# First attention of an eight-block kernel: the scores are computed once, lessened by the row minimum and turned by transposes

## The reference, cut to what matters

```python
q = einsum('ed,bdw->bew', Wq, qp) + bq[:, None]      # 64 rows = 8 heads of 8
k = einsum('ed,bdw->bew', Wk, qp) + bk[:, None]
val = einsum('ed,bdw->bew', Wv, vp) + bv[:, None]    # vp: patches of the context
scores = einsum('bhdi,bhdj->bhij', qh, kh) / sqrt(8)
scores = where(mp[:, :, None, :] > 0, scores, -1e9)
attn = softmax(scores, axis=-1)
o = gelu(einsum('bhij,bhdj->bhdi', attn, vh), approximate=False)
out = (einsum('de,bew->bdw', Wo, o) + bo[:, None]) * masks
```

## Time and profile before

| | |
|---|---|
| median of 3 runs (lowest, highest) | 1655.13 us (1654.13, 1655.79) |
| the profiled execution's own time | 1655.96 us |
| its span, first to last instruction | 1654.2 us |
| busy in the span: PE / DVE / ACT / POOL | 89% / 59% / 33% / 32% |
| mean granted TensorE clock | 0.974 |
| first attention: first score matmul / last copy of outputs | starts at 56.6 us / starts at 357.7 us |

### The profile page before, as it was taken

The page is one execution under the profiler, slowest core; times in us unless marked ns, Lnnn a source line. Parts: engine busy times, 40 slices in busy tenths (PEclk is TensorE's granted clock), DMA queues, the critical chain, the costliest instruction groups (busy, mean ns, idle before and its releaser), DMA issues.

```text
span 1654.2 us, 20269 instructions
## 1 busy us (share of the span) xinstructions
PE 1477.4 (89%) x6854; PEld 1055.1 (64%) x6854; DVE 981.1 (59%) x2158; ACT 547.8 (33%) x1414; POOL 531.9 (32%) x531
## 2 busy tenths in 40 slices
PE   0788888877888989999899998899999999999898
PEld 0344444434766677676678776777777777777555
DVE  2565666655768334888322245677777777777543
ACT  1223222233342213454323113334434334434332
POOL 4100000004523232341312113545545545443163
PEclk9999999999999979999899999999999999999799
DMA  5111111112313210010111104111111111110001
GB/s 157 53 39 37 33 32 33 28 36 90 96 58 102 64 51 1 8 33 1 39 39 51 39 1 147 32 58 51 46 58 51 46 58 51 46 48 4 7 1 51
DMA packets 63481, 77.52 MB, mean 47 GB/s; under 512 B 7138, under 2 KB 34018, under 8 KB 63252
## 3 DMA queue, kind: packets, MB, share of 16 engines
q1 hardware_dynamic: 62416, 74.99, 14.9%
q10 hardware_dynamic: 964, 1.25, 0.2%
HBM read 57.34 MB, written 10.49 MB: 41 GB/s over the span
## 4 chain that ended last, share of the span: by engine, by line
PE 70%; DVE 12%; issue 5%; POOL 4%; SPq 4%; DMA 3%; ACT 2%; POOLq 0%; DVEq 0%; ACTq 0%
PE bank L423 15%; PE bank L428 14%; PE bank L427 14%; SPq L910 3%; PE bank L2331 3%; PE bank L1961 2%; PE bank L2309 2%; PE bank L1950 2%; PE bank L2224 2%; DMA ring_l<-k 2%; PE bank L1959 2%; PE bank L2206 2%; PE bank L490 1%; DVE xn L1807 1%; PE bank L2318 1%
## 5 line engine op out<-in xcount | busy, mean ns | idle before, releaser
L1012 POOL TENSOR_TENSOR ring_l<-stage,ring_h 128x512 fp32r<-128x512 f32 x133 | 179.0, 1363 | 235.6 <-ACT ring_h L1168 235.6
L423 PE MATMUL bank<-xTh_b,ring_h 128*128 128x512 f32 x464 | 191.3, 412 | 2.8 <-issue 1.5
L427 PE MATMUL bank<-xTl_b,ring_h 128*128 128x512 f32 x464 | 185.4, 400 | 0.0
L428 PE MATMUL bank<-xTh_b,ring_l 128*128 128x512 f32 x464 | 185.2, 399 | 0.0
L1119 POOL TENSOR_TENSOR q<-xn 128x512 f32<-128x512 f32 x64 | 82.2, 1284 | 220.6 <-DVE xn L1807 220.6
L423 PE MATMUL bank<-ring_h,o3h 128*128 128x512 f32 x256 | 125.7, 491 | 0.8 <-issue 0.8
L1446 ACT ACTIVATE probs<-bank,nbias 128x128 f32<-128x128 f32 x256 | 90.5, 366 | 54.7 <-DVE nbias L1831 54.7
L1437 ACT ACTIVATE probsT<-bank 128x512 f32<-128x512 f32 x64 | 38.3, 598 | 205.6 <-PE bank L2318 205.6
L423 PEld LDWEIGHTS bank<-xTh_b,ring_h 128*128 128x128 f32 x464 | 88.8, 191 | 23.2 <-issue 4.4
L428 PEld LDWEIGHTS bank<-xTh_b,ring_l 128*128 128x128 f32 x464 | 88.5, 191 | 21.7
L428 PE MATMUL bank<-ring_h,o3l 128*128 128x512 f32 x256 | 101.0, 395 | 0.0
(11 more groups left out here) (327 smaller groups left out, 3535.0 us busy)
## 6 DMA issues: line engine op xcount, KB each, us to landing
stage<-in_units_dram SPq DMA_DIRECT2D x133, 256.0 KB, 3.2
ring_h<-q SPq DMA_DIRECT2D x64, 64.0 KB, 2.0
ring_l<-k SPq DMA_DIRECT2D x64, 64.0 KB, 2.1
raw_k<-kvs SPq DMA_DIRECT2D x16, 256.0 KB, 2.1
raw_v<-kvs SPq DMA_DIRECT2D x16, 256.0 KB, 2.0
kraw<-raw_k SPq DMA_DIRECT2D x16, 256.0 KB, 3.4
v<-raw_v SPq DMA_DIRECT2D x16, 256.0 KB, 3.0
stage<-in_context_dram SPq DMA_DIRECT2D x8, 256.0 KB, 3.1
```

The source lines that it names most:

```text
L423: ins = nc.tensor.matmul(out_ap, wh, mh, start=start, stop=False)
L427: nc.tensor.matmul(out_ap, wh, ml, start=False, stop=False)
L428: return nc.tensor.matmul(out_ap, wl, mh, start=False, stop=stop)
L1012: nc.gpsimd.tensor_tensor(ring_l[:, place_of(u), :], stage[:, u % STAGE, :], f32(ring_h[:, place_of(u), :]), ALU.subtract).then_inc(w_lo, 1)
```

## The change

The turned scores, `q0b` with its DMAs, `pick4`, `mB` and the whole handling of the maxima go. The queries are copied with scale -1, so that `scores0` gives negated scores, and the row maximum becomes a row minimum. In each step the differences to that minimum are written to `probs` in SBUF: in even steps by VectorE (one 128 x 512 subtraction behind its reduction), in odd steps by ScalarE (four 128 x 128 activations, one for each head). `turned0` then turns the tile by four transposes, two steps behind the scores, and one exponential follows, with the sign put right by its scale. Queries and keys are made one group ahead instead of two. The order of the steps is one loop over l = 4g + p in each engine's list.

```diff
-            sp.wait_ge(su_zero, 2)
+            sp.wait_ge(su_zero, 1)
             for g in range(G0):
-                sp.wait_ge(a0_ev, at0(g, "q"))
-                if g >= 2:
-                    sp.wait_ge(a0_st, 4 * (g - 2) + 4)
-                blocks0(q0b, q0[:, g % 2, :], g, s_q0b)
                 sp.wait_ge(a0_ev, at0(g, "k"))
                 if g >= 2:
                     sp.wait_ge(a0_s, 4 * (g - 2) + 4)
                 blocks0(k0b, k0[:, g % 3, :], g, s_k0b)
...
-            nc.gpsimd.memset(q0b.bitcast(F32), 0.0).then_inc(su_zero, 1)
...
+            def lessened0(n):
+                a.wait_ge(a0_mx, n // 2 + 1)
+                if n >= 3:
+                    a.wait_ge(a0_tr, n - 2)
+                for h in range(4):
+                    c = slice(h * P, (h + 1) * P)
+                    ins = nc.scalar.activation(probs[:, n % 3, c], bank[n % 2][:, c], ACT.Identity, scale=-1.0,
+                                               bias=nbias[:, n % 4, h:h + 1])
+                ins.then_inc(a0_sa, 1)
+
+            for l in range(4 * G0 + 4):
+                g, p = l // 4, l % 4
+                if 2 <= l < 4 * G0 + 2:
+                    exponentials0(l - 2)
+                if l < 4 * G0 and on_act0(l):
+                    lessened0(l)
+                if p == 3 and g >= 1:
+                    outputs0(g - 1)
+                if p == 0 and g + 1 < G0:
+                    queries0(g + 1)
+                if p == 1 and g + 1 < G0:
+                    keys0(g + 1)
...
+            def least0(n):
+                v.wait_ge(a0_s, n + 1)
+                rows4 = by_tile(bank[n % 2][:])
+                if on_act0(n):
+                    if n >= 4:
+                        v.wait_ge(a0_sa, n // 2 - 1)
+                    nc.vector.tensor_reduce(nbias[:, n % 4, :], rows4, AX.X, ALU.min).then_inc(a0_mx, 1)
+                    return
+                link(v, v_chain, nc.vector.tensor_reduce(nbias[:, n % 4, :], rows4, AX.X, ALU.min))
+                if n >= 3:
+                    v.wait_ge(a0_tr, n - 2)
+                nc.vector.tensor_tensor(by_tile(probs[:, n % 3, :]), rows4, nbias[:, n % 4, :].unsqueeze(2).to_broadcast((P, 4, P)),
+                                        ALU.subtract).then_inc(a0_sd, 1)
...
+            for l in range(4 * G0 + 4):
+                g, p = l // 4, l % 4
+                if l < 4 * G0:
+                    least0(l)
+                if p == 1 and g >= 2:
+                    normalized0(g - 2)
+                if p == 3 and g % 2 == 0 and g + 2 < G0:
+                    low_qk0((g + 2) // 2)
+                top(1 if p == 3 else 2)
...
-                nc.tensor.matmul(bank[2 + n % 2][:], k0[:, g % 3, c], q0b[:, g % 2, p, :, :], start=True, stop=False)
-                t.wait_ge(a0_mb, g + 1)
-                nc.tensor.matmul(bank[2 + n % 2][:].rearrange("j (h i) -> j h i", h=4), pick4[:, p, :], mB[:, g % 2, :, :],
-                                 start=False, stop=True).then_inc(a0_st, 1)
+            def turned0(n):
+                ready0(t, n)
+                if n >= 2:
+                    t.wait_ge(a0_e, n - 1)
+                for h in range(4):
+                    c = slice(h * P, (h + 1) * P)
+                    ins = nc.tensor.transpose(bank[2 + n % 2][:, c], probs[:, n % 3, c], ident[:, :])
+                ins.then_inc(a0_tr, 1)
...
+            for l in range(4 * G0 + 3):
+                g, p = l // 4, l % 4
+                if l < 4 * G0:
+                    scores0(g, p)
+                if 2 <= l < 4 * G0 + 2:
+                    turned0(l - 2)
+                if p == 0 and g >= 2:
+                    turned_outputs0(g - 2)
+                if l >= 3:
+                    outputs0((l - 3) // 4, (l - 3) % 4)
+                if p == 0 and g + 1 < G0:
+                    queries0(g + 1)
+                if p == 1 and g + 1 < G0:
+                    keys0(g + 1)
+                if p == 2 and g % 2 and g + 1 < G0:
+                    values0((g + 1) // 2)
+                if p == 2 and g % 2 == 0 and g + 2 < G0:
+                    projection0((g + 2) // 2)
```

More of the change, by code:

```diff
@@ L98, in constants @@
         place[b, b, 24::32] = 1
-    rep = np.concatenate([rep.reshape(P, 8 * P), np.zeros((P, 8 * P), np.float32)], 1)
-    rep[:32, 8 * P:8 * P + 512] = pick4.reshape(32, 512)
-    return {"rep": rep, "block4": block4, "place": place, "con": con, "ident": np.eye(P, dtype=np.float32), "tabs": tabs,
+    rep = rep.reshape(P, 8 * P)
+    return {"rep": rep, "place": place, "con": con, "ident": np.eye(P, dtype=np.float32), "tabs": tabs,
             "iota": np.broadcast_to(np.arange(512, dtype=np.float32), (P, 512)).copy()}
@@ L268, in program @@
         scol = sb("scol", [P, 32], F32, e0)
+        scol_n = sb("scol_n", [P, 32], F32, e0)
         bcol = sb("bcol", [P, 32], F32, e0)
         ones0 = sb("ones0", [P, P], F32, e0)
-        mraw = sb("mraw", [P, 16], F32, e0)
-        mhl = sb("mhl", [P, 32], F32, e0)
         rsum0 = sb("rsum0", [P, 16], F32, e0)
@@ L527, in program @@
         a0_mx = sem("a0_mx")
[L528 to L531, removed]
+        a0_sd = sem("a0_sd")
+        a0_sa = sem("a0_sa")
+        a0_tr = sem("a0_tr")
         a0_e = sem("a0_e")
@@ L542, in program, with on_act0, ready0 @@
         G0 = 2 * B
+        def on_act0(n):
+            return n % 2 == 1
+        def ready0(eng, n):
+            eng.wait_ge(a0_sa if on_act0(n) else a0_sd, n // 2 + 1)
         def at0(g, kind):
@@ L1241, in _ @@
             a.wait_ge(su_mk, 3)
[L1242 to L1265, removed]
@@ L1266, in _, with exponentials0 @@
-            outputs0(G0 - 1)
+            def exponentials0(n):
+                at = 4 * (n // 8) + n % 4
+                a.wait_ge(a0_tr, n + 1)
+                if n >= 3:
+                    a.wait_ge(a0_pv, n - 2)
+                nc.scalar.activation(probsT[:, n % 3, :], bank[2 + n % 2][:], ACT.Exp, bias=bcol[:, at:at + 1],
+                                     scale=(scol if on_act0(n) else scol_n)[:, at:at + 1]).then_inc(a0_e, 1)
+            def lessened0(n):
[7 more added lines that the diff above has]
+                ins.then_inc(a0_sa, 1)
@@ new lines, in _ @@
+            for l in range(4 * G0 + 4):
[13 more added lines that the diff above has]
+                if p == 2 and g % 2 == 0 and g + 2 < G0:
+                    high0((g + 2) // 2)
+                if p == 3 and g % 2 and (g - 1) // 2 + 2 < B:
+                    inputs0((g - 1) // 2 + 2)
+                if p == 3 and g in (3, 4):
+                    hi.upto(g - 2)
@@ L1582, in _ @@
             low_qk0(0)
-            for g in range(-1, G0):
-                for p in range(4):
-                    if g + 1 < G0:
-                        maximum0(g + 1, p)
-                    if p == 0 and g >= 1:
-                        normalized0(g - 1)
-                    if p == 2 and g % 2 and g + 3 < G0:
-                        low_qk0((g + 3) // 2)
-                    if p < 3:
-                        top(2)
-                if g + 1 < G0:
-                    halves0(g + 1)
-                    top(1)
-                    blocks_of_max0(g + 1)
-                if g % 2 == 1 and (g + 1) // 2 + 3 < B:
-                    b = (g + 1) // 2 + 3
+            for l in range(4 * G0 + 4):
[7 more added lines that the diff above has]
+                top(1 if p == 3 else 2)
+                if p == 3 and g % 2 == 0 and g // 2 + 3 < B and g:
+                    b = g // 2 + 3
                     v.wait_ge(a0_c, b - 3)
```

83 lines of the change are left out of this document (14 added, 69 removed).

## The result

| | before | after | forecast |
|---|---|---|---|
| median, us (lowest to highest, 4 runs each) | 1655.38 (1654.13 to 1655.79) | 1538.78 (1538.50 to 1540.84) | 1581.5 (1562 to 1603) |
| ratio to before, 95% interval | | 0.9296 (0.9285 to 0.9308) | 0.956 |
| profiled span, us | 1654.2 | 1536.6 | |
| first score matmul starts at | 56.58 | 50.73 | 50.3 |
| last copy of outputs starts at | 357.65 | 241.44 | 284 |

The kernel is 7.0% faster. It takes 43 us less than was forecast, and the time lies outside the range. The span is 117.6 shorter: 5.9 at the start, 110.4 in the groups (301.1 before, 190.7 after), 1.4 behind them. The forecast had 6.3, 67.4 and 0. So the whole miss lies in the groups, and the time is that of rival C, which I had given 8 in 100.

The account below looks back on a forecast made before the run. TensorE at 1.2 GHz was to bound the groups: 14.2 us of work plus a 0.8 stall, 15.0 each. Groups 67.4 less and start 6.3 less made 73.7 us gained, so 1581.5 us, range 1562 to 1603.

Parts of the forecast that it names:

- rival C: First attention's groups: TensorE's clock rises as gaps vanish, VectorE binds at some 12.2 us a group, 1540 us; chance 0.08.
- I price everything at 1.2 GHz: First attention: TensorE's clock stays at the low level after the change, giving 14.2 us of its work a group.
- Start: Before the groups: q0b's memset, earlier key DMAs and smaller loads save 6.3 us (3.5 to 8.1).
- Transposes: Four transposes in each step on TensorE: 0.80 us, with 0.71 and 1.06 as ends.
- (b): Step 0 of a group: TensorE waits for ScalarE's copy of the outputs, a new stall of 0.8 us, counting in full.
- (c): Keys made in step 1 for the next group: usable at 8.5, needed at 10.2, hidden with 1.7 us to spare.
- B: A new wait takes more, nearest the keys 2.9 us later than counted: 16.2 us a group, 1599 us; chance 0.14.
- E: Slower: the keys' loop becomes the bound; with keys 6.8 us late the time is 1662 us; chance 0.02.
- (d): VectorE's queue in a group: 11.8 us of work against TensorE's 15.0, small lateness taken by two steps of slack.
- Behind the groups: What follows the first attention is not touched and moves forward as it is, with 0 us gained there.
- D: ScalarE's and VectorE's handshakes pace each step: groups stay at about 19.2 us, only the start is won, 1649; chance 0.04.

Follow-up runs that it names:

- the control on 128 rows: Kernel after, each score product of the first attention issued twice, both on all 128 rows: 1546.9 us, 8 more.
- the reordering: Kernel after, ScalarE's copy of the outputs put ahead of its four activations in step 3: 1536.2 us, ratio 0.9278.

## Why the prediction was wrong

**The step that failed is TensorE's clock.** "I price everything at 1.2 GHz" multiplied a correct list of work by the wrong level. Its ground was that 12.5 us without a gap had stayed low. That reading is right, and the trace of the run with scores on 32 rows repeats it over 60 us. The conclusion was not: I took a property of those steps for one of the stage. Each of the four steps held a product on 32 rows, L1961 in the earlier trace rows, and the change removes exactly these. Its form "32*128" stands in the row. The run from the kernel before with the wider product and the three from the kernel after show that the rows of products, at equal columns, move the clock: with the product widened to 128 rows it rises where it never did, and 41 us are won, in part by closer matmuls; with a narrow product in each step, narrowed or added, it stays down for tens of microseconds, and 34 to 38 are lost, while the control on 128 rows loses 8. A narrow product does two things at once: it uses fewer rows, and it keeps the weight loads of itself and of the next product from starting early (0.72 to the next start, against 0.42). Through which of the two it holds the clock down, no run separates.

I also looked at the wrong feature of the earlier trace rows, 512-column matmuls that follow one another directly. In the kernel after the clock rises in a run of scores, four transposes and outputs, with 512-column products on all 128 rows at most three times in a row, as the prediction had counted.

The Trainium skill ("TensorE: Matmul & The Clock Gate", What's actually happening) says that the gate goes by how busy the array has been. In the kernel after waits of 1.1 us or more stand ahead of each fall (1.31 and 1.22 in the group shown), which agrees with that. The 59.87 busy of 60 us at 1.2 GHz don't, if busy is what the profile counts as busy. I had set its advice against the trace and dropped it; each held half: falls come behind gaps, as the traces show without an experiment on gaps alone, and narrow products keep the clock low without any.

**How much of the miss is the clock.** The run with scores on 32 rows comes near the forecast, 1576.3 against 1581.5, but isn't quite the forecast's kernel. At 1.2 GHz its narrow scores and the transposes behind them cost 0.73 + 1.05 a step (164.97 to 165.70, and 170.34 to 171.39), those of the kernel after 0.59 + 0.98, so 0.8 of its 15.3 a group comes from the rows directly. In part it runs at the high level, which makes it faster than the forecast's kernel would be. By estimate a group at 1.2 GHz throughout, with full rows, takes 15.3 - 0.8 = 14.5, and 16 times the 2.8 from there to 11.7 is 45 us. The miss was 43: the clock accounts for all of it, as far as this estimate goes.

Point by point:

- **Start**: forecast 6.3 (3.5 to 8.1), measured 5.9. Right. The first projection starts at 39.18 instead of 44.01, 4.8 earlier, which holds the memset of 3.5 and the smaller loads; the key issue adds the rest.
- **Transposes**: forecast 0.80 between 0.71 and 1.06, measured 0.98 at 1.2 GHz (60.20 to 61.18). Mis-sized, near the upper end that the earlier trace rows showed as a duration.
- **(b), the stall for the turned outputs**: forecast 0.8 a group, measured 16.1 in 15, 1.1 each (the 3.3 of the forecast is 3.4 by its own terms). Place and cause right, size near. That it "counts in full" did not hold: in the kernel after the reordering moved the time by 3 or nothing, and by 8 once VectorE had less to do. At 1.2 GHz the longer transposes cover most of it (3.8 in 4 waits in the run with scores on 32 rows), as the prediction said that it shrinks as they grow.
- **(c), the keys**: hidden with 1.7 to spare at 15.0 a group. In the run at 15.3 a group this holds. In the kernel after the group is 3.3 shorter, the slack is spent, and TensorE waits 20.6 in 14, 1.5 each. The wait costs little as VectorE binds; rivals B and E had it as the bound, and here it is not.
- **(d), VectorE**: 11.8 a group. Measured: groups of 11.7 with VectorE busy at 19.6 of 20 us. Right to 0.1. Rival C, which names the mechanism that came, had 12.2 a group "with its waits" and 1540, and 1538.8 was measured. That it is so close is partly luck: 14 groups at 11.7 are 7 us less than it counted, and the first and last groups took about 6 more.
- **Behind the groups**: moved forward as a block, 1.4 less in it. Right.
- **The rivals B, D, E** didn't come: no group at 16 or more, handshakes hidden, the start won as said.

Open is why the clock in the run with the 32-row product added is high in one stretch and low in the next, with the same steps in it. The runs show that rows move it, and the traces that it falls behind gaps, but no rule that gives its level from the instruction list.

## What to carry to other kernels

Read the level of TensorE's clock from the durations, then ask what in the instruction mix keeps it there, rows per product among it, and whether the change takes that away; if it might, price both levels and let the engine that binds at the high one give the second forecast. When another engine's account comes near the bound, write down the time at which it would take over: here that line was right to 2 us, partly by luck. A stall of an engine is worth its length only if that engine binds; the order of a list that is worth nothing today can be worth 8 us after the real bound has moved.

## What the runs showed of the hardware

- A product on 32 rows has the same duration as one on 128 (0.79 and 0.80 in the earlier trace rows), yet costs more in a stream: the next starts 0.72 later at 1.2 GHz, against 0.42 for the same product on 128 rows (165.27 to 165.69). And the clock stays low with it. Widening 64 products from 32 to 128 rows with zeros made a kernel of 1655 us faster by 41, by both effects together.
- TensorE can be busy for 59.87 of 60 us, as the profile counts it, and stay at 1.2 GHz (the run with scores on 32 rows, 140 to 200 us).
- The granted clock reads 1.00 at the start of a profile, while matmuls last 0.80 and 0.63; in the kernel after it reads 1.00 from 60 to 80 us, across the rise at 65.5. It can be trusted from the first change of level on (0.50 with 0.63, in the run with scores on 32 rows).
- Four transposes of 128x128 (fp32) take 0.98 to the next start at 1.2 GHz and 0.53 at 2.4 (60.20 to 61.18; 67.90 to 68.43).
